# A graph layer on one core: the histogram's one-hots in one comparison a chunk, and POOL's gathers without two waits

## The reference, cut to what matters

```python
row, col = src, dst                       # 50000 nodes, 50000 edges; dst is sorted
h    = silu(concat([x[row], x[col], edge_attr]) @ eW1 + eb1)
m_ij = silu(h @ eW2 + eb2)
agg  = segment_sum(m_ij, row, num_segments=50000)
upd  = silu(concat([x, agg]) @ nW1 + nb1) @ nW2 + nb2
out  = layernorm(x + (x + upd))
```

## Time and profile before

| | us |
|---|---|
| median of 3 runs | 1612.81 |
| lowest, highest | 1610.55, 1620.77 |
| span of the profiled execution | 1611.9 |
| median less that span | 0.9 |
| busy in the span: PE, PEld | 1213.7, 873.1 |
| busy: DVE, ACT, POOL | 780.3, 458.8, 1023.1 |

### The profile page before, as it was taken

The page is one execution under the profiler, slowest core; times in us unless marked ns, Lnnn a source line. Parts: engine busy times, 40 slices in busy tenths (PEclk is TensorE's granted clock), DMA queues, the critical chain, the costliest instruction groups (busy, mean ns, idle before and its releaser), DMA issues.

```text
span 1611.9 us, 24482 instructions
## 1 busy us (share of the span) xinstructions
PE 1213.7 (75%) x6825; PEld 873.1 (54%) x6825; DVE 780.3 (48%) x3182; ACT 458.8 (28%) x846; POOL 1023.1 (63%) x1267
## 2 busy tenths in 40 slices
PE   1224487778788787888878887877877869999995
PEld 1224255545455454555555544544545559888884
DVE  7448434433443434434344333333333439888885
ACT  0000111122222222222222221211222227777775
POOL 7471745555556565555555665666666548998996
PEclk9999888999999999999988997998999979999998
DMA  9991443456666566565555655654655349999994
GB/s 379 413 413 40 134 151 119 135 159 191 186 186 198 176 189 190 178 191 182 182 183 178 181 177 155 183 179 142 195 168 166 90 138 399 411 413 412 411 406 180
DMA packets 175501, 352.97 MB, mean 219 GB/s; under 512 B 30350, under 2 KB 81855, under 8 KB 175364
## 3 DMA queue, kind: packets, MB, share of 16 engines
q1 hardware_dynamic: 128740, 230.97, 43.4%
q10 hardware_dynamic: 21600, 68.32, 10.6%
q0 software_dynamic: 25024, 52.10, 10.2%
HBM read 235.21 MB, written 116.06 MB: 218 GB/s over the span
## 4 chain that ended last, share of the span: by engine, by line
PE 41%; another core or an unknown queue 19%; issue 15%; DVE 7%; POOL 6%; ACTq 6%; DMA 3%; ACT 1%; POOLq 0%; SPq 0%; DVEq 0%
PE psum L658 11%; ACTq L763 6%; PE psum L702 5%; PE psum L681 4%; PE psum L732 4%; PE psum L704 4%; PE psum L689 3%; DMA ring<-table 3%; PE psum L700 3%; PE psum L714 3%; PE psum L646 3%; POOL windows L613 2%; PE psum L747 2%; DVE same L993 2%
## 5 line engine op out<-in xcount | busy, mean ns | idle before, releaser
L539 POOL DMA_INDIRECT table<-qs,pos x391 | 387.8, 992 | 361.6 <-DVE qs L1021 262.5
L496 POOL DMA_INDIRECT ring<-x_d,idx_src x391 | 380.5, 973 | 169.9 <-issue 117.8
L658 PE MATMUL psum<-work,windows 128*128 128x128 f32 x1568 | 241.6, 319 | 173.3 <-issue 164.7
L658 PEld LDWEIGHTS psum<-work,windows 128*128 128x128 f32 x1568 | 228.6, 229 | 244.3 <-issue 244.3
L977 DVE COPY work<-psum 128x512 f32<-128x512 f32 x98 | 67.8, 691 | 471.4 <-remote 300.1
L732 PE MATMUL psum<-work,ring 128*128 128x80 f32 x1250 | 157.5, 280 | 26.6 <-DVE work L1041 22.4
L732 PEld LDWEIGHTS psum<-work,ring 128*128 128x128 f32 x1250 | 149.6, 196 | 35.4 <-issue 22.7
L1021 DVE COPY qs<-psum 128x512 f32<-128x512 f32 x98 | 67.6, 690 | 188.2 <-remote 174.9
L681 PE MATMUL psum<-xT_in,w_self 128*128 128x320 f32 x314 | 128.7, 495 | 24.4 <-issue 19.6
L784 ACT COPY u_out<-psum 128x320 f32<-128x320 f32 x129 | 54.9, 426 | 290.4 <-remote 242.5
L773 ACT COPY work<-psum 128x512 f32<-128x512 f32 x98 | 57.4, 586 | 277.2 <-PE psum L658 194.3
(11 more groups left out here) (120 smaller groups left out, 1572.0 us busy)
## 6 DMA issues: line engine op xcount, KB each, us to landing
windows<-x_d SPq DMA_DIRECT2D x392, 128.0 KB
ring<-table SPq DMA_DIRECT2D x79, 528.0 KB, 10.6
table<-empty ACTq DMA_DIRECT2D x9, 4224.0 KB
edge_rows<-edges_dram SPq DMA_DIRECT2D x98, 384.0 KB
xT_in<-xT_d SPq DMA_DIRECT2D x78, 320.0 KB
out<-windows ACTq DMA_DIRECT2D x78, 320.0 KB, 6.1
u_dram<-u_out SPq DMA_DIRECT2D x64, 320.0 KB
own_x<-x_d SPq DMA_DIRECT2D x48, 320.0 KB, 8.3
```

The costliest lines, as they stand in the source:

```text
L496: pool.indirect_dma_start(rows, None, x[:, :], bass.IndirectOffsetOnAxis(ap=idx[:, g * TILES + t:g * TILES + t + 1], axis=0)).then_inc(don ...
L539: pool.indirect_dma_start(table[:, :], bass.IndirectOffsetOnAxis(ap=pos[:, g * TILES + t:g * TILES + t + 1], axis=0), q[g % Q][:, t, :], None,
L658: last = nc.tensor.matmul(p_dst[:, t * P:(t + 1) * P], window[g % WINDOWS][:, t, r * D:(r + 1) * D], pick[g % 2][:, r, t * P:(t + 1) * P], ...
```

## The change

DVE compares a whole chunk in one `tensor_tensor`: 14 columns of coarse values, broadcast over 125, against a constant pattern `chunk_ids` (each of the 125 numbers 14 times, f16, made by POOL with an `iota`). The coarse values are first copied to f16 (`coarse_h`). The layout of a chunk turns from (column, coarse) to (coarse, column), so that a column's one-hot, PE's stationary operand, now has a step of 14 elements. `own_homes` shrinks to one chunk, so HOMES is 17. POOL's two waits go, with `PAUSES`.

```diff
-PAUSES = 11, 20
...
-            coarse_ids = tmp("coarse_ids", [P, COARSES], F16)
+            chunk_ids = tmp("chunk_ids", [P, COARSES * CHUNK], F16)
+            coarse_h = tmp("coarse_h", [P, COLS], F16)
...
-            own_homes = tmp("own_homes", [P, 2 * CHUNK * COARSES], F16)
+            own_homes = tmp("own_homes", [P, CHUNK * COARSES], F16)
...
-                               (own_homes, 4 * CHUNK * COARSES)):
+                               (own_homes, 2 * CHUNK * COARSES)):
             for k in range(bytes_in // (2 * CHUNK * COARSES)):
-                is_coarse.append(tile[:, k * CHUNK * COARSES:(k + 1) * CHUNK * COARSES].rearrange("p (c f) -> p c f", f=COARSES))
+                is_coarse.append(tile[:, k * CHUNK * COARSES:(k + 1) * CHUNK * COARSES].rearrange("p (f c) -> p f c", c=CHUNK))
...
             pool.iota(bucket_i[:], [[1, COARSES]], base=0, channel_multiplier=0).then_inc(s_iota, 1)
+            pool.iota(chunk_ids[:], [[1, COARSES], [0, CHUNK]], base=0, channel_multiplier=0,
+                      allow_small_or_imprecise_dtypes=True).then_inc(s_chunk_ids, 1)
...
             for g in range(X_SRC):
-                if g == PAUSES[0]:
-                    pool.wait_ge(s_count_mm, COLS // CHUNK - HOMES)
-                if g == PAUSES[1]:
-                    pool.wait_ge(s_count_mm, COLS // CHUNK)
                 gather_src(g)
...
-                last = nc.tensor.matmul(p_count[c // BANK_COLS][0:COARSES, o:o + FINE], is_coarse[c // CHUNK % HOMES][:, c % CHUNK, :],
+                last = nc.tensor.matmul(p_count[c // BANK_COLS][0:COARSES, o:o + FINE], is_coarse[c // CHUNK % HOMES][:, :, c % CHUNK],
                                         is_fine[:, c, :], start=True, stop=True)
...
-            V.tensor_copy(coarse_ids[:], bucket_i[:]).then_inc(s_plan, 1)
+            V.tensor_copy(coarse_h[:], coarse[:, 0:COLS]).then_inc(s_plan, 1)
             dve.wait_ge(s_plan, 17)
-            for c in range(COLS):
-                if c % CHUNK == 0 and c >= HOMES * CHUNK:
-                    dve.wait_ge(s_count_mm, c // CHUNK - HOMES + 1)
-                last = V.tensor_scalar(is_coarse[c // CHUNK % HOMES][:, c % CHUNK, :], coarse_ids[:], coarse[:, c:c + 1], None,
-                                       ALU.is_equal)
-                if c % CHUNK == CHUNK - 1:
-                    last.then_inc(s_is_coarse, 1)
+            dve.wait_ge(s_chunk_ids, 1)
+            for k in range(COLS // CHUNK):
+                if k >= HOMES:
+                    dve.wait_ge(s_count_mm, k - HOMES + 1)
+                cols = coarse_h[:, k * CHUNK:(k + 1) * CHUNK]
+                V.tensor_tensor(is_coarse[k % HOMES], chunk_ids[:].rearrange("p (f c) -> p f c", c=CHUNK),
+                                cols.unsqueeze(1).to_broadcast([P, COARSES, CHUNK]), ALU.is_equal).then_inc(s_is_coarse, 1)
```

More of the change, by code:

```diff
@@ L200, in gnn_kernel @@
             sem(n) for n in ("s_idx_src", "s_idx_dst", "s_src_i", "s_dst_i", "s_weights"))
-        s_slot_i, s_iota, s_consts, s_ident, s_empty, s_fill = (
-            sem(n) for n in ("s_slot_i", "s_iota", "s_consts", "s_ident", "s_empty", "s_fill"))
+        s_slot_i, s_iota, s_chunk_ids, s_consts, s_ident, s_empty, s_fill = (
+            sem(n) for n in ("s_slot_i", "s_iota", "s_chunk_ids", "s_consts", "s_ident", "s_empty", "s_fill"))
         s_plan, s_ids, s_is_fine, s_is_coarse, s_count_mm, s_sums, s_before_tile, s_worst, s_fit_mm, s_fits_i = (
```

## The result

The changed kernel takes 1629.33 us (median of 10 runs, 1622.71 to 1637.49) against 1615.35 us for the kernel before (10 runs): ratio 1.0085, interval [1.0061, 1.0110]. That is 14 us slower and inside the 1% that I had set as the bound. The profiled span is 1628.9 us, 17.0 us above that of before. Of my cases the forecast (+8) and C (+18) lie next to it, C the nearer one.

A forecast was written before the change was run, and what follows sets the result against it. Main loop and node phase have no slack, so the plan's end, with PE starved beside fill and gathers, sets the time. First scatter 2 us later plus 6 for strided weights: +8 us, about 1620 us; range 1558 to 1655.

The forecast's parts named there:

- the forecast: Likeliest case for the whole kernel: +8 us, about 1620 us, own range 1607 to 1633; chance 0.43.
- C: Rival: PE starved as long as POOL gathers, release only at 146 us; +10 on the forecast, 1630 us; chance 0.11.
- DVE's comparison: In the plan, one f16 comparison over 128x1750 per chunk takes 1.1 us, against DVE's present 2.28 us.
- POOL's iota, "cost nothing": At the start, ahead of the first gather: the larger iota takes about 1.67 us, within POOL's slack, costing nothing.
- Starved from 31 us: PE's histogram runs at full pace from about 22.5 to 31 us, 5 chunks done, then starves.
- Starved PE: an instruction every 0.7 us where DVE asks for none: PE's histogram while starved: 0.7 us an instruction, 1.4 where DVE asks too; 4 chunks in 107 us.
- Ended by the fill at 126 us, a backlog later, 138: PE's starving ends a backlog after the table fill, between 133 and 146 us, taken as 138.
- Tail: PE's last 19 chunks (266 columns) after starving: 30 us, plus 6 us for strided weights (bounds 0 to 30).
- Rival B: PE's strided weight loads at half rate: about 30 us on the tail, 3 us more; +35 us, 1647 us; chance 0.24.
- A check later by 9 us, given back but for 2: Plan checked at 172 us against 162.64; check to first scatter 40.5 us against 48; first scatter 212.5, 2 us later.
- A shifted start shifts the end: Main loop and node phase have no slack, so a shifted start moves the end by about as much.
- my 168: Forecast time in us at which PE's counts end in the plan, instead of 155.6.

The follow-up runs named there:

- e5: The changed kernel with chunks of 7 columns instead of 14 (weights' step 14 bytes), on the 1325 kind of chip: 1335.51 us, one run.
- e2: The kernel before with only POOL's two waits removed, comparisons and packed weights as before: 1637.94 us, ratio 1.0155.
- e4: The changed kernel with chunks of 4 columns instead of 14 (weights' step 8 bytes): 1621.38 us, one run.
- e10: The changed kernel with two waited-for memsets behind each of POOL's first 104 gathers, on the 1615 kind: 1609.91 us, one run.
- e1: The changed kernel with POOL's two waits put back (groups 11 and 20): 1622.07 us, ratio 1.0051.
- e3: The changed kernel with one-hots in the old layout (column, coarse): one comparison a chunk, packed weights, no large iota, no waits: 1586.68 us, ratio 0.983.
- e9: The changed kernel itself run again, on the 1615 kind of chip: 1634.79 us, ratio 1.0138.
- e8: e3 with POOL gathering 18 groups ahead of the first scatter instead of 28, on the 1325 kind: 1364.79 us, ratio 1.0295.
- e7: The changed kernel with two waited-for memsets behind each of POOL's first 104 gathers, on the 1325 kind: 1387.09 us, one run.

## Why the prediction was right, and which terms were not

The time (1629 against 1620), a change of under 1% and the range held. The state that I had read from the earlier trace rows, PE starved beside POOL's gathers, did set the end of the plan. But the sum came out by luck: its terms erred by 12 to 28 us one way and the other. The case whose number (1630) and whose release of PE came true is C, to which I had given 0.11.

*DVE's comparison.* 1.07 us, as taken.

*POOL's iota, "cost nothing".* 4.50 us, not 1.67, with DVE's cast stretched beside it. I took the price of an element from an iota of one partition whose innermost step is 2; this one has 128 partitions and an innermost step of 0, and e5's with 875 elements took 2.65 us. It delayed the fill by 4.7 us and the first gather by 5.6 us (4.06 to 9.69). So it did not cost nothing: the last gather, which came to decide the end of the starving, was later by it.

*Starved from 31 us.* This step failed most. I had it begin nine microseconds after PE's start whatever DVE did. On the 1615 kind it begins when gathers have come 1.25 to 1.32 us apart for ten to twenty microseconds: at 30 us before, in e2 and in e4, and at 81 us after, 20 us behind the end of the long comparisons, which had stretched the gathers to 1.96 and then about 1.5 us apart. e10, where memsets keep them 1.71 us apart when no comparison is left, is never starved in the plan. Whether it would begin without the fill no run of this kind shows. When the starving began at 81 us, 247 columns (17 chunks and 9) were done, not 70. (The Trainium skill, page SBUF — State Buffer, section Who interferes with whom, says that a DVE operation with two inputs in SBUF contends with an operation of POOL's that reads SBUF, and that the port pair which they share is an exclusive lock. The rows agree that a gather lengthens beside it, 0.94 to 1.66 us; no row shows a port.)

*Starved PE: an instruction every 0.7 us where DVE asks for none.* It stayed at 1.4 us with DVE silent, as in the earlier trace rows with DVE busy. From 80.6 to 165.8 us PE did 36 columns, one in 2.4 us. My reading of "one thing every 0.7 us" for PE and DVE together was wrong: silence of DVE's gave PE nothing.

*Ended by the fill at 126 us, a backlog later, 138.* Ended by the gathers, 11.8 us after the last of them. The last gather ended at 154.0 us and not at about 140, since the first was 5.6 us late and the comparisons stretched some twenty more; in e2, with neither, it ended at 137.7 us. And the 5.9 us that I had read as the time to release is longer after longer runs of gathers: 5.9 us after 44 and after 36 of them (before), 8.1 after 80 (e1), 9 to 14.5 after 104 (e3, the change, e4, e2). Here rival C was right, and my argument against it, that with gathers alone from 155.9 to 161 us nothing starved, took five microseconds after a pause of 30 us for a steady state: the onset needs more.

*Tail.* I had 266 columns at the packed price, 30 us, and 6 us for the stride. There were 109, in 24.4 us, of which the stride is half: 12 us. Rival B's mechanism, the doubling, was right, and I had weighed it low. e4 and e5 grade it: packed 0.112 us a column, a step of 8 bytes 0.122, 14 bytes 0.203, 28 bytes 0.227. (By the rule on 16-byte lines in the Trainium skill, page SBUF — State Buffer, section Specifications (TRN2), the term would have been at its upper bound, and the traces agree.) B's price fell short of its 33 us because fewer columns were left. But the stride has a second price that I had not seen: 392 columns at 0.227 us take 89 us and run into the starving at 81 us, where packed ones (e3) end at 77 us. Between the change and e3, which also does without the large iota, lie 110 us at the check of the plan and 43 us in the total (2.5% by the ratios, 1.0085 and 0.983).

*A check later by 9 us, given back but for 2.* It was 31.5 us later, and 21.3 us were given back: 26.7 us from check to first scatter. With the gathers over, nothing stalls, as I had said. But my 40.5 had 37 for the work itself, and that price was wrong: I took seven products of 512 columns at the 2.07 us of the earlier trace rows, and they take 1.1 us here. The same product before and after, each followed by the stretch of 10 us that it lies in or next to (busy time of POOL's gathers and their number, granted clock, DMA share, GB/s):

```profile
197.03 2.07 PE L714 MATMUL psum<-work,w_e 128*128 128x512 f32 x2 [6.83 <-ACT work L790]
190.00:200.00 10.00, 4.77 (x6) 0.50 0.38 111
```

```profile
212.00 1.10 PE L712 MATMUL psum<-work,w_e 128*128 128x512 f32 x2
200.00:210.00 10.00, 1.25 (x2) 1.00 0.68 199
```

Before, PE had done next to nothing since 187.5 us when the granted clock fell to 0.50 (1.2 GHz) at 190 us; in the change PE worked without a gap from 165.8 to 190.2 us and the clock stays at 1.00. Seven products at 1.1 us save 6.8 us of my 14.5 and the window products (3.62, 1.95 and 1.95 us) 3 of my 10.5: 37 becomes 27. The clock is not all of it: three products between 175 and 184 us took 2.07 us, too, where the profile before gives 1.00. e2 and e9, where PE counts columns until shortly before the check and the gathers are over, have 26.5 and 27.1 us; e1, with gathers beside its first groups, has 49.9.

*A shifted start shifts the end.* Half right. +10.1 us at the first scatter became +17.0 in the profiled span; over all runs of the 1615 kind the length of the loop between first and last scatter varies from 1085 us (e10, 214.4 to 1299.8) to 1102 us (e1, 213.6 to 1315.3) without a cause that I can name, so that the last 7 us stay unexplained. (Before, the loop ends at 1302.6 us, not at about 1290.)

Net: the counts ended at 190.2 us, 22 us past my 168: 28 for the later release, 12 for the stride, less 18 for 157 columns fewer at 0.112 us. Of that the path to the first scatter gave back 14 us more than I had taken (40.5 less 26.7). So it came 8 us past my 212.5, or 2 us past it with the 6 us for the stride, which the forecast held beside it. Errors of 40 us one way (28 and 12) met 32 us the other (18 and 14), and that they cancelled is luck.

What stays open: why issue starves under dense gathers on one kind of chip and not on the other (the instruction queues q8 and q14 moved 135 packets of 175499 in the whole run and none from 81 to 165 us, so it is not a load of instructions that these rows show, and nothing else in the profile names the cause); and what the change and e3 do on the 1325 kind, which was not run. The nearest to the change there, e5, took 1335.51 us in its one run, 10 us over the kernel before.

## What to carry to other kernels

When an idle engine's releaser is "issue" and the gaps are all equal (1.4 us here), look at what another engine issues at that time and how densely, and when the state began and ended, to the microsecond; test it with a dummy instruction that spaces that engine. Here the comparison merged from 14 into one was a gain only with a layout that leaves the matmul's stationary operand packed: pay on DVE (1.98 against 1.07 us a chunk), where PE then waits 0.24 us a chunk, rather than on PE (1.65 against 3.16). When a term is taken from rows of a stretch with stalls, ask whether the engine ran at its full clock there: a product took 2.07 us in it and 1.1 us outside. And measure on more than one chip before POOL's order is tuned: pauses against starving have nothing to act on where it doesn't occur. e8, packed and with fewer gathers ahead, costs 3% there, and e7, whose memsets end the starving on the one kind (e10), took 1387.09 us against 1325.03 on the other.

## What the runs showed of the hardware that I had not expected

- The same program takes 1614 to 1615 us on two chips and 1325 to 1326 us on two others. On the 1615 kind PE falls to one instruction in 1.4 us after 10 to 20 us of gathers 1.25 to 1.32 us apart, and in the kernel before DVE does, too; 1.71 us apart (one run, e10) they did no harm in the plan. PE comes back 6 to 14.5 us after the last gather.
- Granted 0.50 of the clock, two matmuls of 512 f32 columns take 2.07 us before; at 1.00 they take 1.1 us in the change. Three before that took 2.07 us with 1.00 granted remain unexplained.
- An f16 weight load of 125 columns with its matmul takes 0.112 us packed, 0.203 us at a step of 14 bytes and 0.227 us at 28.
- A f16 `tensor_tensor` over 1750 elements takes 1.07 us with its broadcast outside and 1.98 us with the broadcast innermost.
- A f16 iota of 1750 elements in 128 partitions with a zero step takes 4.50 us beside a small cast of DVE's, which took 5.12 us in place of 0.46.
